# 25 output chunks moved into the last image, four kinds of steps, and a new order of exponentials and turns in an attention kernel

## The reference

```python
xn = group_norm(x, 32 groups)
q, k, v = split(xn @ qkv_w.T + qkv_b)             # per pixel, 256 channels each
# 7 x 7 regions of 8 x 8 pixels per image; each region looks at its 4 best regions
q_r, k_r = mean over each region of q, k
idx = top_k(q_r @ k_r.T, 4)
for each of 49 regions, 8 heads of 32 channels:
    attn = softmax(q * 256 ** -0.5 @ k[idx].T)     # 64 queries x 256 keys
    out = attn @ v[idx]
lepe = depthwise 3 x 3 convolution of v, + bias
return x + (out + lepe) @ out_w.T + out_b
```

## Time and profile before

| | |
|---|---|
| median of three runs | 1802.1 us (1801.96 to 1802.63) |
| profiled execution | 1803.27 us |
| its span, first to last instruction | 1801.4 us |
| PE, DVE, ACT, POOL busy | 95%, 84%, 81%, 61% |
| mean granted clock of PE | 0.991 |
| HBM read and written | 155.33 and 51.38 MB |

### The profile page before, as it was taken

The page is one execution under the profiler, slowest core; times in us unless marked ns, Lnnn a source line. Parts: engine busy times, 40 slices in busy tenths (PEclk is TensorE's granted clock), DMA queues, the critical chain, the costliest instruction groups (busy, mean ns, idle before and its releaser), DMA issues.

```text
span 1801.4 us, 76163 instructions
## 1 busy us (share of the span) xinstructions
PE 1708.4 (95%) x26568; PEld 1384.0 (77%) x26568; DVE 1517.6 (84%) x3329; ACT 1466.7 (81%) x4793; POOL 1097.6 (61%) x2464
## 2 busy tenths in 40 slices
PE   4999999999999999999999999999999999988886
PEld 4878887888878887788878888788887888766664
DVE  6478988898988898898888898889897888888884
ACT  1478888888878888788888888788887888877775
POOL 3256666666656666666666666666665666555542
PEclk9999999999999999999999999999999999999999
DMA  5323434343434444344443343434343434332332
GB/s 183 87 83 109 145 113 136 102 137 115 143 100 127 125 127 123 116 130 124 128 121 120 117 137 116 130 105 145 107 134 89 119 103 123 97 116 87 105 95 84
DMA packets 157016, 211.66 MB, mean 117 GB/s; under 512 B 17888, under 2 KB 144736, under 8 KB 156640
## 3 DMA queue, kind: packets, MB, share of 16 engines
q1 hardware_dynamic: 141408, 129.71, 24.9%
q0 software_dynamic: 15232, 77.08, 12.9%
HBM read 155.33 MB, written 51.38 MB: 115 GB/s over the span
## 4 chain that ended last, share of the span: by engine, by line
PE 70%; ACT 15%; DVE 9%; issue 4%; DMA 0%; POOL 0%; ACTq 0%; POOLq 0%; DVEq 0%
PE chunk_bank L848 20%; PE pt_bank L932 15%; PE s_bank L919 12%; ACT probs L501 11%; PE o_bank L946 9%; PE chunk_bank L862 8%; DVE neg_max L699 4%; DVE lepe L603 3%; PE chunk_bank L877 2%; PE o_bank L956 2%; ACT probs_t L508 2%; ACT v_stage L475 1%; ACT q_all L484 1%; PE s_bank L848 1%; PE s_bank L895 1%
## 5 line engine op out<-in xcount | busy, mean ns | idle before, releaser
L501 ACT ACTIVATE probs<-s_bank,neg_max 128x256 f32<-128x256 f32 x1568 | 737.4, 482 | 190.2 <-DVE neg_max L699 189.9
L699 DVE TENSOR_REDUCE neg_max<-s_bank 128x2 f32<-128x512 f32 x784 | 506.0, 685 | 158.0 <-PE s_bank L919 157.0
L328 POOL COPY k_sel<-k_all 128x128 f32 x1568 | 403.9, 299 | 377.0 <-PE s_bank L919 354.9
L603 DVE SCALAR_TENSOR_TENSOR lepe<-v_band,taps,lepe 128x448 f32<-128x448 f32 x896 | 608.4, 725 | 0.0
L848 PE MATMUL chunk_bank<-xn,wqkv 128*128 128x224 f32 x2544 | 570.6, 357 | 2.5 <-DVE xn L639 2.5
L508 ACT COPY probs_t<-pt_bank 128x512 f32<-128x512 f32 x784 | 464.5, 593 | 71.2 <-PE pt_bank L932 70.5
L932 PE MATMUL pt_bank<-ident,probs 128*128 128x128 f32 x3136 | 498.1, 282 | 11.8 <-ACT probs_t L508 11.6
L848 PEld LDWEIGHTS chunk_bank<-xn,wqkv 128*128 128x128 f32 x2544 | 442.6, 192 | 11.7 <-DVE xn L639 2.6
L932 PEld LDWEIGHTS pt_bank<-ident,probs 128*128 128x128 f32 x3136 | 358.5, 141 | 70.9 <-ACT probs_t L508 19.0
L339 POOL TENSOR_TENSOR lepe<-o_norm,lepe 128x128 f32<-128x128 f32 x392 | 255.3, 651 | 187.3 <-DVE o_norm L717 186.8
L501 ACT ACTIVATION_READ_ACCUMULATOR probs<-s_bank,neg_max 128x1 f32 x1568 | 330.6, 211 | 0.0
(11 more groups left out here) (69 smaller groups left out, 1196.1 us busy)
## 6 DMA issues: line engine op xcount, KB each, us to landing
v_sel<-v_dram SPq DMA_DIRECT2D x1568, 64.0 KB
xn<-x_dram POOLq DMA_DIRECT2D x56, 448.0 KB, 4.9
v_dram<-v_stage SPq DMA_DIRECT2D x112, 224.0 KB
resid<-x_dram POOLq DMA_DIRECT2D x56, 448.0 KB, 4.3
out_dram<-resid POOLq DMA_DIRECT2D x56, 448.0 KB, 3.3
wqkv<-w_qkv_dram SPq DMA_DIRECT2D x1, 768.0 KB, 9.8
wout<-w_out_dram SPq DMA_DIRECT2D x1, 256.0 KB, 12.4
idx_row<-top_idx SPq DMA_DIRECT2D x8, 0.8 KB
```

The lines of the kernel that those rows point to most:

```text
L328: last = pool.tensor_copy(k_sel[:, r % K_SLOTS, :, RT * j:RT * (j + 1)], k_all[:, b % 2, :, bass.ds(reg[j] * RT, RT)])
L501: act.activation(probs[:, u, :], s_bank[:, u, 0:KEYS], ACT.Exp, bias=neg_max[:, r % 2, u:u + 1], accum_out=denom[:, r % 2, u:u + 1]).then_ ...
L603: ins = dve.scalar_tensor_tensor(row, v_band[:, n % BANDS, k, t // 3:t // 3 + RS, t % 3:t % 3 + W], taps[:, k, t:t + 1], row, ALU.mult, AL ...
L699: dve.tensor_reduce(neg_max[:, r % 2, 2 * hf:2 * hf + 2], s_bank[:, 2 * hf:2 * hf + 2, 0:KEYS], AX.X, ALU.max, negate=True).then_inc(max_d ...
```

## The change

**Chunks moved.** For 25 rows the second half of the output chunk is not made in the step after the row. POOL writes the row's `lepe` buffer to a DRAM tensor `spill` (`spill_row`), loads and stores only the first half of its `resid`, and the second half is made in the last image's steps: `load_late` brings three (or two) rows back into ring places of `xn` that are no longer in use, `load_late_x` the matching x into a part of `k_all` that is no longer in use, `project_late` makes the chunk, `late_half` adds bias and x, `store_late` stores it.

**Four kinds of steps** besides the full one: short (a late row goes before it), first and last of an image, and tail (the last image). Each has its own order of projection calls on PE, evictions on ACT and units on DVE.

**Region means** get a place in the ring of chunk banks (`"rm"`) in place of the corner of `s_bank`, and are made in parts. On DVE `image_stats` stands ahead of two taps and `normalize_o` ahead of `image_var` and `image_scale`.

**Order in an iteration.** On PE the first turns stand behind the scores. On ACT the evictions come first, then the copy of the first turns, the four exponentials in one run, the copy of the second turns, and the reciprocals.

```diff
+TAIL = ROWS - NWIN
+LATE_GROUPS = ((5, 12, 19), (26, 33, 40), (6, 13, 20), (27, 34, 41), (8, 15, 22), (29, 36, 43), (10, 17),
+               (24, 31, 38), (45, 47))
+LATE = [g for group in LATE_GROUPS for g in group]
+LATE_AT = {TAIL: (0,), TAIL + 1: (1,), TAIL + 2: (2,), TAIL + 3: (3,), TAIL + 4: (4,), TAIL + 5: (5, 6),
+           TAIL + 6: (7, 8)}
...
+def step_kind(s):
+    if s >= TAIL:
+        return "tail"
+    if s % NWIN == 0:
+        return "first"
+    if s % NWIN == LAST:
+        return "last"
+    return "short" if s - 1 in LATE else "full"
...
+    if kind == "first":
+        return [v0, ("rm", n, 0), v1, k0, k1, q0, o0, vt0, vt1, q1]
+    if kind == "last":
+        return [v0, v1, k0, vt0, vt1, k1, o0, q0, q1]
+    if kind == "short":
+        return [v0, v1, k0, k1, o0, vt0, vt1, q0, q1]
+    if kind == "full":
+        return [v0, v1, k0, k1, o0, o1, vt0, vt1, q0, q1]
+    late = [("late", g, 1) for g in late_rows(s)]
+    return late[:3] + [o0, o1, q0, q1] + late[3:]
...
 # POOL
+            def spill_row(g):
+                pool.wait_ge(o_row_done, NWIN * (g + 1))
+                pool.dma_start(spill[LATE.index(g)], lepe[:, :, g % LEPE_RING, :]).then_inc(spilled, 16)
...
+                for k in range(KC):
+                    pool.dma_start(xn[:, k, late_set(i), :], spill[at:at + len(group), :, k, :].rearrange(
+                        "i p r -> p i r")).then_inc(late_in[i % LATE_SETS], 16)
...
+                    elif rc == 4:
+                        for i in LATE_AT.get(s + 1, ()):
+                            load_late(i)
+                    elif rc == 6:
+                        for i in LATE_AT.get(s + 1, ()):
+                            load_late_x(i)
...
 # ACT, one iteration
-                    if is_region(r):
-                        probs_t_out(r, 0)
-
...
+                    if is_region(r):
+                        probs_t_out(r, 0)
                     if is_region(r + 1):
-                        exp(r + 1, 0)
-                        exp(r + 1, 1)
+                        for u in range(HG):
+                            exp(r + 1, u)
                     if is_region(r):
                         probs_t_out(r, 1)
-                    if is_region(r + 1):
-                        exp(r + 1, 2)
-                        exp(r + 1, 3)
-                    if rc == 1 and first and is_row(kv):
-                        qk_means_out(kv // NWIN)
                     if is_region(r):
                         recips_out(r)
...
 # DVE, one iteration
                     if is_region(r + 1):
                         maximum(r + 1, 1)
+                    if is_region(r - 1):
+                        normalize_o(r - 1)

                     if rc == 2 and ends_x:
                         image_var(xr // NWIN)
                     elif rc == 4 and ends_x:
                         image_scale(xr // NWIN)

-                    if is_region(r - 1):
-                        normalize_o(r - 1)
-
+                    if kind == "tail":
+                        if rc < 5:
+                            outer_tap(now, 2 * rc)
+                            outer_tap(now, 2 * rc + 1)
...
+                        if rc < 3 and late:
+                            late_half(late[rc])
...
 # PE, one iteration
                     if is_region(r):
-                        turn_probs(r, 0)
                         pe.wait_ge(exp_done, HG * (r + 1))

-                    if rc == 1 and first and is_row(kv):
-                        region_means(kv // NWIN)
-                    elif rc == 2 and first and is_row(kv):
+                    if rc == 3 and kind == "first":
                         affinities(kv // NWIN)
...
                     if is_region(r + 1):
                         scores(r + 1)
+                    if is_region(r):
+                        turn_probs(r, 0)
                     if is_region(r - 1):
                         attend(r - 1)
                     if is_region(r):
                         turn_probs(r, 1)

-                    if rc == 0:
-                        project("v", kv, 0, 0, 4)
+                    if kind == "tail":
+                        if rc < 3 and late:
+                            project_late(late[rc], 0, 2)
+                        elif rc in (3, 4):
+                            project_out(s - 1, rc - 3, 0, 2)
...
+                    elif rc == 0:
+                        project("v", kv, 0, 0, 4 if kind in ("full", "first") else 2)
```

More of the change, by code:

```diff
@@ L89, in put @@
     def put(chunks, banks):
-        keys = [(kind, n, k) for kind, n in chunks if is_row(n) for k in range(2)]
-        for i, key in enumerate(keys):
+        for i, key in enumerate(chunks):
             places[key] = (i % banks, used[i % banks])
@@ L195, in side, with late_set, late_place, late_dram @@
             return s_bank[:, HG - 1, KEYS + at:KEYS + at + n]
+        late_x = k_all[:, 0, :, :].rearrange("p k t -> p (k t)").rearrange("p (i r) -> p i r", r=ROW)
+        def late_set(i):
+            first = LATE_SLOTS * (i % LATE_SETS)
+            return slice(first, first + len(LATE_GROUPS[i]))
+        def late_place(g):
+            i = next(i for i, group in enumerate(LATE_GROUPS) if g in group)
+            return i, LATE_SLOTS * (i % LATE_SETS) + LATE_GROUPS[i].index(g)
+        def late_dram(rows, i):
+            group = LATE_GROUPS[i]
+            return rows[group[0]:group[-1] + 1:group[1] - group[0], :, 1, :].rearrange("i p r -> p i r")
         def bank_of(kind, n, k):
@@ L827, in _ @@
                     else:
-                        for i in range(12, KC * (TAPS - 1)):
-                            outer_tap(now, i)
+                        if kind == "full":
+                            outer_tap(now, 12)
+                        outer_tap(now, 13)
+                        outer_tap(now, 14)
+                        outer_tap(now, 15)
         @block.tensor
@@ L865, in project_out, with project_late @@
                     ins.then_inc(full("out", g, m), 1)
+            def project_late(g, first, last):
+                place_i, slot = late_place(g)
+                for i in range(first, last):
+                    half, part = divmod(i, KC)
+                    cols = slice(HALF * half, HALF * (half + 1))
+                    if i == 0:
+                        pe.wait_ge(late_in[place_i % LATE_SETS], 16 * KC * (place_i // LATE_SETS + 1))
+                        wait_bank(pe, "late", g, 1)
+                    ins = pe.matmul(bank_of("late", g, 1)[:, cols], wout[:, part, P:2 * P], xn[:, part, slot, cols],
+                                    start=(part == 0), stop=(part == KC - 1))
+                if last == QUARTERS:
+                    ins.then_inc(full("late", g, 1), 1)
             def turn_v(n, m):
@@ L1057, in _ @@
                     elif rc == 3:
-                        if not last_row:
+                        if kind == "first":
+                            project("k", kv, 1, 1, 3)
+                        elif kind == "full":
                             project_out(s - 1, 0, 2, 4)
+                        else:
+                            project("k", kv, 1, 2, 4)
                     elif rc == 4:
-                        if last_row:
+                        if kind == "first":
+                            project("q", qn, 0, 2, 4)
+                        elif kind == "last":
```

346 lines of the change are left out of this document (253 added, 93 removed).

## The result

The changed kernel takes 1841.4 us (median of four runs, 1840.7 to 1842.5), the kernel before 1802.0 in the same job: ratio 1.0219, 95% interval 1.0201 to 1.0237. It is slower by 2.2%, 39 us; the forecast was 1839.

The account below looks back on a forecast made before the run. PE was taken to bound full steps, a 4.00 us circle through scores and exponentials the last image. Full +43, short +3, image-end pairs -11 and smaller terms: +36, taken as +37; 1803.3 + 37 - 1.2 = 1839 us, range 1815 to 1862.

Parts of the forecast that it names:

- PE's order, +0.30 per region: PE in some 390 regions: +0.16 waiting for ACT's copy of the first turns, +0.14 for first turns behind scores.
- the choice of 0.58 over 0.44: First turns behind scores on PE: taken at 0.58 us, as behind attend, not 0.44 as behind a projection; +0.14.
- How the wait shows: In a full step, PE idle for 0.1 to 0.2 us ahead of second turns, released by ACT's copy of pt_bank.
- ACT's floor: Circle of scores, maximum, exponentials and copy that sets every region's least period: to fall from 4.00 to 3.7 us (3.71).
- Ends of images: Six pairs of last and first steps: 63.3 us against 65.05 per pair, -1.8 each, together -11.
- The waits that I kept at 0.5 us: PE's waits at an image's end (0.29 means, 0.35 o_norm, 0.55 region means' eviction): mostly go, 0.5 us kept.
- Tail: Last image's steps: late chunks cost nothing, filling time where PE waits; six steps +1, the seventh +1; clock stays up.
- The DMA term: Late loads in the seven tail steps: bounds 0 and +17 us, taken as 0 since DMA engines are a third busy.
- The faster rival: Second turns do not wait for the copy: 1777 us, or 1784 or 1722 in its variants; chance 0.30.
- The slower one: An eviction delays ACT's first copy: wait grows by up to 0.4 in two regions of seven, 1883 us; chance 0.13.

## Why the prediction was right

- *PE's order, +0.30 per region.* Right in sum and in both parts. Periods came out as 4.16, 4.54 and 4.60 against 4.15, 4.53 and 4.59; full steps +42.8 against +43, short ones +4.2 against +3. The shortened copy splits the sum into the 0.16 and 0.15 that the rows had given. First turns behind scores, which the trace before did not show, take 0.60, so the choice of 0.58 over 0.44 was right; the run with a call ahead of attend shows that the price belongs to the return to full tiles and not to attend.
- *How the wait shows.* I expected idle PE of 0.1 to 0.2 us ahead of the second turns. 0.10 shows as idle; the other 0.06 of the 0.16 is that the turns no longer begin under attend's tail. Whoever had looked for the whole 0.30 as idle PE would not have found it: PE's busy share is 95% before and after.
- *ACT's floor.* 3.79 measured with the order alone, 3.71 forecast. In a region with four calls it does not decide, since PE's own chain, 4.16, is longer.
- *Ends of images.* Mis-sized: the six pairs gave -15.2, not -11. The waits that I kept at 0.5 us went nearly all: in the last step shown above PE is idle for 0.66 us of 30.43, no more than in a full step (0.64 of 31.52).
- *Tail.* The chunks cost next to nothing themselves (+1.8 over five steps), and the clock stays at 1.00 up to the stalls, both as forecast. The DMA term was mis-sized: I took 0 from bounds of 0 to +17, and the two steps with five chunks lost about 10 us, by another way than I had named: it was not the late rows that came late, but the gather of v behind them.
- *Prologue.* -2.8 where I had 0. The order alone has it too (-2.8) and the old order with moved chunks has not (-0.2), but the run with spread loads, whose prologue and order are the changed kernel's, has only -1.0. So part of it varies between executions; what the rest is was not looked into.

These misses (-4, +10, -3) nearly cancel. That the total lies within 3 us is in part luck: the main term is right by its mechanism, the smaller ones offset each other. The faster rival falls with the chain of the changed kernel, where second turns wait for ACT's copy, and with the shorter copy, which takes this wait away. The slower one, ACT late for the first copy, falls too: ACT waits 0.94 us for the turns in the region above.

## What to carry to other kernels

When a buffer has one copy, count what lies between its two uses before moving either of them: here 1.2 us of other PE work covered a 0.67 us hand-over and 0.58 us did not. Lowering a floor is worth nothing while another engine's own list is longer, and two edits in one change should be priced apart: one of these gains 37 us and the other loses 77. Group PE work by tile shape: in these traces each return from small tiles to the full array has a price of 0.14 to 0.20 us.

## What the runs showed of the hardware

- A projection call right behind tiles of 32 rows or columns takes 0.57 to 0.58 us against 0.38, four turns 0.59 against 0.44. The difference is about one weight load (0.192 and 0.141 us on the mean), and behind such tiles the load starts with its matmul instead of ahead of it.
- A wait of 4.3 us on PE was followed by half clock: 0.50 from 1766 to 1770, a mean of 0.76 over the 8 us around it, with attend at 1.08 us in place of 0.65.
- In the kernel before, the granted clock fell to a mean of 0.88 in a tail step with no wait of that length; in the changed kernel's first five tail steps it is 1.00.
